# First loads under semaphores of their own, and a last stage in column halves of 290, in a one-core adapter, attention and expert kernel

## Time and profile before

| | us |
|---|---|
| median of 3 runs | 1396.19 (1395.92 to 1399.05) |
| the profiled execution | 1395.68 |
| its span in the profile | 1393.9 |
| TensorE busy in the span | 1328.4 (95%) |
| VectorE busy | 1068.3 (77%) |
| ScalarE busy | 861.1 (62%) |
| GpSimd busy | 655.9 (47%) |

### The profile page before, as it was taken

The page is one execution under the profiler, slowest core; times in us unless marked ns, Lnnn a source line. Parts: engine busy times, 40 slices in busy tenths (PEclk is TensorE's granted clock), DMA queues, the critical chain, the costliest instruction groups (busy, mean ns, idle before and its releaser), DMA issues.

```text
span 1393.9 us, 26480 instructions
## 1 busy us (share of the span) xinstructions
PE 1328.4 (95%) x8088; PEld 1138.0 (82%) x8088; DVE 1068.3 (77%) x2951; ACT 861.1 (62%) x2499; POOL 655.9 (47%) x652
## 2 busy tenths in 40 slices
PE   4889997799999999999999999999999999999988
PEld 3666665588888888888888888888888888888877
DVE  3677866478888888888888888888888888888855
ACT  1567776466666676666666666676666667666631
POOL 1345546453545363536453654365345535453511
PEclk9799998999999999999999999999999999999999
DMA  7445444444121212121212122312212121213121
GB/s 259 146 149 159 158 153 140 134 114 114 31 66 37 80 32 62 31 77 32 61 32 77 31 61 41 82 40 51 71 38 61 32 76 32 61 31 73 28 74 61
DMA packets 193520, 107.59 MB, mean 77 GB/s; under 512 B 140897, under 2 KB 178274, under 8 KB 191970
## 3 DMA queue, kind: packets, MB, share of 16 engines
q1 hardware_dynamic: 192224, 105.38, 28.1%
q10 hardware_dynamic: 1154, 0.50, 0.1%
HBM read 101.66 MB, written 37.75 MB: 100 GB/s over the span
## 4 chain that ended last, share of the span: by engine, by line
PE 81%; SPq 10%; DVE 3%; issue 3%; DMA 2%; ACT 1%; POOL 0%; DVEq 0%; ACTq 0%; POOLq 0%
PE ps L1168 11%; PE ps L1170 11%; PE ps L1169 11%; PE ps L1219 10%; PE ps L1240 5%; PE ps L1233 5%; PE ps L1234 5%; SPq L79 5%; PE ps L1253 4%; SPq L80 4%; PE ps L1252 4%; PE ps L1259 4%; PE ps L1195 2%; PE ps L236 1%; PE ps L892 1%
## 5 line engine op out<-in xcount | busy, mean ns | idle before, releaser
L1365 ACT ACTIVATE b_pf<-b_sm,b_nb,b_rstd 128x640 f32<-128x640 f32 x256 | 235.2, 919 | 102.4 <-DVE b_nb L1470 102.2
L1371 ACT ACTIVATE b_p_h<-ps 128x640 fp32r<-128x640 f32 x256 | 180.3, 704 | 180.3 <-PE ps L1219 179.6
L1484 DVE TENSOR_TENSOR b_p_l<-ps,b_p_h 128x640 fp32r<-128x640 f32 x256 | 210.7, 823 | 82.9 <-ACT b_p_h L1371 75.8
L1463 DVE CUSTOM_DVE_ANT_0 b_sm<-ps,mask_row 128x640 f32<-128x640 f32 x256 | 209.3, 817 | 2.7 <-PE ps L1170 2.0
L1219 PE MATMUL ps<-ident,b_pf 128*128 128x128 f32 x1280 | 182.8, 274 | 10.0 <-DVE b_p_l L1484 8.0
L1479 DVE TENSOR_SCALAR b_pf<-b_pf,b_ri 128x640 f32<-128x640 f32 x256 | 159.0, 621 | 27.7 <-DVE b_ri L1476 0.5
L1168 PE MATMUL ps<-b_w_h,x1t_h 128*128 128x512 f32 (+1 forms) x512 | 179.2, 350 | 0.5 <-DVE b_qt_l L1451 0.5
L1219 PEld LDWEIGHTS ps<-ident,b_pf 128*128 128x128 f32 x1280 | 152.9, 141 | 29.6 <-issue 10.1
L1168 PE MATMUL ps<-b_kt_h,b_qt_h 128*128 128x320 f32 x512 | 174.6, 341 | 1.0 <-DVE b_mx L1463 1.0
L1169 PE MATMUL ps<-b_w_l,x1t_h 128*128 128x512 f32 (+1 forms) x512 | 173.4, 339 | 0.0
L1170 PE MATMUL ps<-b_w_h,x1t_l 128*128 128x512 f32 (+1 forms) x512 | 172.8, 337 | 0.0
(11 more groups left out here) (163 smaller groups left out, 3237.0 us busy)
## 6 DMA issues: line engine op xcount, KB each, us to landing
kv_of_batch<-in_kv SPq DMA_DIRECT2D x128, 256.0 KB
b_ck<-kv_of_batch SPq DMA_DIRECT2D x64, 256.0 KB, 3.6
b_cv<-kv_of_batch SPq DMA_DIRECT2D x256, 64.0 KB, 2.2
raw<-in_w SPq DMA_DIRECT2D x32, 384.0 KB, 5.4
raw<-in_wo SPq DMA_DIRECT2D x32, 256.0 KB, 3.6
a_xt<-in_xt SPq DMA_DIRECT2D x8, 256.0 KB, 5.1
a_xin<-in_x SPq DMA_DIRECT2D x8, 256.0 KB, 5.2
x<-a_x SPq DMA_DIRECT2D x8, 256.0 KB, 5.2
```

The costliest lines, as they stand in the source:

```text
L1365: act.activation(pf[:, h % 2], sm[:, h % 2], ACT.Exp, bias=nb[:, m.b % 2, h:h + 1], scale=rstd[:, m.b % 4, h:h + 1], accum_out=rs[:, m.b % ...
L1371: act.activation(p_h[:, :, h * P:(h + 1) * P], turned_row, ACT.Copy).then_inc(ph_sb, 1)
L1463: dve.tensor_tensor_reduce(sm[:, h % 2], score_row, mask_row[:, m.b], 1.0, MASKED, ALU.add, ALU.max, mx[:, k, h:h + 1]).then_inc(mx_sb, 1)
L1484: dve.tensor_tensor(p_l[:, :, cols], turned_row, p_h[:, :, cols], ALU.subtract).then_inc(pl_sb, 1)
```

## The change

At the start: `la`, `lb`, `b_cond` and four column blocks of 128 of `wc` have semaphores of their own, and low_rank(0), cond(0) and y_out(0) wait for what they read. `wq` is loaded as its first 512 columns (with the small arrays, under `qkv_in`) and its last 256 (`kv_in`). ScalarE's queue issues the inputs of the choice first, then runs a small activation on zeros into `scrap`, then issues `pages` and the tables' inputs. `key_row` moves to SyncE's queue, behind `wq`'s last columns. The eight mask rows leave `table_angles`: four are made between kv_out(0) and rope_sum(0), four after `table_products` in slot 0.

In the last stage: `W3 = 580` columns are cut at `CUT = 290`. `gate(b)` makes columns 290 to 579: 222 output columns and the 68 of gate and `low`. `rest(b)` makes columns 0 to 289. `add_low_rank` writes all 512 output columns in the outputs' bank, in two pairs (290 and 222 columns). VectorE gets `add_second`, which adds the 222 columns to `hacc`, and does `low_rest(b-1)` ahead of `choose(b)`. The turned `h` has one bank, 6, and the turned `low` has bank 7. `turn(1)` and ScalarE's `h_out(1)` move behind rest(0) and `high(end, 3)`.

The diff, cut to its core:

```diff
             load(0)
-            for part, signal in ((cond_weights, cond_in), (qkv_weights, qkv_in), (rest, rest_in)):
-                for dst, name in part:
-                    sp.dma_start(dst[:], t[name]).then_inc(signal, 16)
+            sp.dma_start(la[:], t["la"]).then_inc(la_in, 16)
+            sp.dma_start(lb[:], t["lb"]).then_inc(lb_in, 16)
+            for o in range(KT):
+                cols = slice(o * P, (o + 1) * P)
+                sp.dma_start(wc[:, :, cols], t["wc"][:, :, cols]).then_inc(wc_in[o], 16)
+            sp.dma_start(b_cond[:], t["b_cond"]).then_inc(b_cond_in, 16)
+            sp.dma_start(wq[:, :, 0:D], t["wq"][:, :, 0:D]).then_inc(qkv_in, 16)
+            for dst, name in qkv_small:
+                sp.dma_start(dst[:], t[name]).then_inc(qkv_in, 16)
+            sp.dma_start(wq[:, :, D:], t["wq"][:, :, D:]).then_inc(kv_in, 16)
+            load_key_row(sp)
+            for dst, name in rest:
+                sp.dma_start(dst[:], t[name]).then_inc(rest_in, 16)
...
                 if a == 0:
-                    pe.wait_ge(cond_in, 16 * len(cond_weights))
+                    pe.wait_ge(la_in, 16)
...
+                if a == 0:
+                    pe.wait_ge(lb_in, 16)
                 for o in range(KT):
+                    if a == 0:
+                        pe.wait_ge(wc_in[o], 16)
...
-            act.dma_start(pages[:], t["pages"]).then_inc(ids_in, 16)
             for dst, name in choice:
                 act.dma_start(dst[:], t[name]).then_inc(adapters_in, 16)
+            act.wait_ge(zero_sb, 1)
+            act.activation(scrap[:], vz[:, 0, 0], ACT.Copy)
+            act.dma_start(pages[:], t["pages"]).then_inc(ids_in, 16)
             load_tables(act)
...
                 if inside(b + 1):
                     kv_out(b + 1)
+                if b == -1:
+                    table_masks(dve, range(4))
...
                 if b == 0:
                     table_products(dve)
+                    table_masks(dve, range(4, B))
...
+    def table_masks(dve, batches):
+
+        dve.wait_ge(key_row_in, 16)
+        for b in batches:
             dve.tensor_scalar(mask_row[:, b], key_row[:], lenf[:, b:b + 1], MASKED, ALU.is_ge, ALU.mult)
...
-    gate_of = lambda b: ps[:, GL[b % 3], 0:NX]
-    lowt_of = lambda b: ps[:, GL[b % 3], P:2 * P]
+    first_of = lambda b: ps[:, F[b % 3], 0:CUT]
+    second_of = lambda b: ps[:, GL[b % 3], 0:CUT]
+    gate_of = lambda b: ps[:, GL[b % 3], D - CUT:CUT]
+    lowt_of = lambda b: ps[:, LT, 0:P]
     rows_of = lambda b: ps[:, F[b % 3], :]
-    HT = (6, 7)
+    HT, LT = 6, 7
...
-        product(pe, b, gate_of(b), slice(D, W3), True).then_inc(gl_ps, 1)
+        product(pe, b, second_of(b), slice(CUT, W3), True).then_inc(gl_ps, 1)
...
-        product(pe, b, rows_of(b), slice(0, D), False).then_inc(f_ps, 1)
+        product(pe, b, first_of(b), slice(0, CUT), False).then_inc(f_ps, 1)
...
-        pe.matmul(rows_of(b), lowt[:, b % 2], bt_h, start=False, stop=False)
-        pe.matmul(rows_of(b), lowt[:, b % 2], bt_l, start=False, stop=True).then_inc(done_ps, 1)
+        for cols in (slice(0, CUT), slice(CUT, D)):
+            pe.matmul(rows_of(b)[:, cols], lowt[:, b % 2], bt_h[:, cols], start=False, stop=False)
+            mm = pe.matmul(rows_of(b)[:, cols], lowt[:, b % 2], bt_l[:, cols], start=False, stop=cols.stop == D)
+        mm.then_inc(done_ps, 1)
...
         turn(pe, 0)
-        turn(pe, 1)
...
         rest(pe, 0)
+        turn(pe, 1)
...
+    def add_second(dve, b):
+        dve.wait_ge(xb_sb, b + 1)
+        dve.tensor_tensor(hacc[:, b, CUT:], second_of(b)[:, 0:D - CUT], hacc[:, b, CUT:], ALU.add)
...
     def rows_dve(dve):
+        add_second(dve, 0)
         for b in range(1, B):
+            low_rest(dve, b - 1)
             choose(dve, b)
...
+            add_second(dve, b)
+            finish(dve, b - 1)
...
             h_out(act, 0)
+            high(end, 3)
             h_out(act, 1)
-            high(end, 3)
             split_b(act)
```

More of the change, by code:

```diff
@@ L95, in phase1 @@
         wq = sb("wq", [P, KT, QKV1])
-        load_tables, table_angles, table_products, table_sines = tables(nc, ctx, memory, t, consts)
+        load_tables, load_key_row, table_angles, table_masks, table_products, table_sines = tables(nc, ctx, memory, t, consts)
         b_qkv = sb("b_qkv", [P, QKV1])
@@ L131, in phase1 @@
         ri = sb("ri", [P, H1])
-        cond_in, qkv_in, rest_in, ids_in = sem("cond_in"), sem("qkv_in"), sem("rest_in"), sem("ids_in")
+        scrap = sb("scrap", [P, 2 * D1])
+        la_in, lb_in, b_cond_in, kv_in = sem("la_in"), sem("lb_in"), sem("b_cond_in"), sem("kv_in")
+        wc_in = [sem(f"wc_in{o}") for o in range(KT)]
+        qkv_in, rest_in, ids_in = sem("qkv_in"), sem("rest_in"), sem("ids_in")
         adapters_in, id_sb, chosen_sb = sem("adapters_in"), sem("id_sb"), sem("chosen_sb")
@@ L156, in context_bank @@
             return M2 if inside(b + 2) else M0
-        cond_weights = ((la, "la"), (wc, "wc"), (lb, "lb"), (b_cond, "b_cond"))
         choice = ((adapters, "adapters"), (ls, "ls"), (which, "which"))
-        qkv_weights = ((wq, "wq"), (b_qkv, "b_qkv"), (cos, "cos"), (sin, "sin"), (ident, "ident"))
+        qkv_small = ((b_qkv, "b_qkv"), (cos, "cos"), (sin, "sin"), (ident, "ident"))
+        QKV_LOADS = 1 + len(qkv_small)
         rest = ((blocks, "blocks"), (causal, "causal"), (wd, "wd"), (b_dense, "b_dense"))
@@ L231, in project_q @@
                 if a == 0:
-                    pe.wait_ge(qkv_in, 16 * len(qkv_weights))
+                    pe.wait_ge(qkv_in, 16 * QKV_LOADS)
                 pe.wait_ge(yt_sb, a + 1)
@@ L239, in project_kv @@
             def project_kv(a):
+                if a == 0:
+                    pe.wait_ge(kv_in, 16)
                 pe.wait_ge(yt_sb, a + 1)
@@ L389, in y_out @@
                 if a == 0:
-                    act.wait_ge(cond_in, 16 * len(cond_weights))
+                    act.wait_ge(b_cond_in, 16)
                 act.wait_ge(yt_ps, a + 1)
@@ L509, in q_out @@
                 if a == 0:
-                    dve.wait_ge(qkv_in, 16 * len(qkv_weights))
+                    dve.wait_ge(qkv_in, 16 * QKV_LOADS)
                 dve.wait_ge(q_ps, a + 1)
@@ L708, in run_gpsimd @@
             pool.wait_ge(zero_sb, 1)
-            pool.wait_ge(qkv_in, 16 * len(qkv_weights))
+            pool.wait_ge(qkv_in, 16 * QKV_LOADS)
             slots(slot)
@@ L735, in tables @@
     cosine = sb("cosine", [P, B, HD // 2])
-    loaded, step, sines = sem("loaded"), sem("step"), sem("sines")
-    loads = ((lens, "lens"), (token, "token"), (inv, "inv"), (norms, "norms"), (key_row, "key_row"))
+    loaded, step, sines, key_row_in = sem("loaded"), sem("step"), sem("sines"), sem("key_row_in")
+    loads = ((lens, "lens"), (token, "token"), (inv, "inv"), (norms, "norms"))
     def load_tables(act):
@@ L741, in load_tables, with load_key_row @@
             act.dma_start(dst[:], t[name]).then_inc(loaded, 16)
+    def load_key_row(sp):
+        sp.dma_start(key_row[:], t["key_row"]).then_inc(key_row_in, 16)
     done = [0]
@@ L763, in table_angles @@
         then(dve, dve.tensor_scalar(angle[:], angle[:], 3.1415925, -3.1415925, ALU.min, ALU.max))
-        for b in range(B):
+    def table_masks(dve, batches):
+        dve.wait_ge(key_row_in, 16)
+        for b in batches:
             dve.tensor_scalar(mask_row[:, b], key_row[:], lenf[:, b:b + 1], MASKED, ALU.is_ge, ALU.mult)
@@ L785, in table_sines @@
         act.activation(half_sine[:], angle[:], ACT.Sin, scale=0.5).then_inc(sines, 1)
-    return load_tables, table_angles, table_products, table_sines
+    return load_tables, load_key_row, table_angles, table_masks, table_products, table_sines
 def phase2_consts(nc, ctx):
@@ L881, in turn @@
     def turn(pe, b):
-        wait(pe, htl_sb, b - 1)
+        wait(pe, htl_sb, b)
         pe.wait_ge(h_sb, DONE - B + b + 1)
         for i in range(KT):
-            mm = pe.transpose(ps[:, HT[b % 2], i * P:(i + 1) * P], hacc[:, b, i * P:(i + 1) * P], ident[:])
+            mm = pe.transpose(ps[:, HT, i * P:(i + 1) * P], hacc[:, b, i * P:(i + 1) * P], ident[:])
         mm.then_inc(ht_ps, 1)
@@ L956, in h_out @@
         wait(act, f_ps, b - 1)
-        act.activation(flat(ht_h[b % 2]), ps[:, HT[b % 2], :], ACT.Copy).then_inc(hth_sb, 1)
+        act.activation(flat(ht_h[b % 2]), ps[:, HT, :], ACT.Copy).then_inc(hth_sb, 1)
     def low_out(act, b):
@@ L975, in h_rest @@
         dve.wait_ge(hth_sb, b + 1)
-        dve.tensor_tensor(flat(ht_l[b % 2]), ps[:, HT[b % 2], :], flat(ht_h[b % 2]), ALU.subtract).then_inc(htl_sb, 1)
+        dve.tensor_tensor(flat(ht_l[b % 2]), ps[:, HT, :], flat(ht_h[b % 2]), ALU.subtract).then_inc(htl_sb, 1)
     def choose(dve, b):
```

8 lines of the change are left out of this document (1 added, 7 removed).

## The result

| | before | changed kernel |
|---|---|---|
| median of the runs taken together | 1396.59 us (4 runs) | 1388.17 us (4 runs, 1387.24 to 1389.66) |
| ratio, 95% interval | | 0.9939 (0.9927 to 0.9952) |
| the profiled execution | 1395.68 us | 1389.66 us |
| its span | 1393.9 us | 1387.9 us |

8.4 us faster, inside the predicted range (1381.5 to 1390.5) and 3.6 us above the number. Five more executions of the same kernel, run later beside other experiments, gave a median of 1387.05 and a ratio of 0.9935 (0.9922 to 0.9949); over all nine executions the median is 1387.65.

What follows compares the result with a forecast made beforehand. Phase 1 was taken as bound by SyncE's queue with 0.8 us of slack, after a latency-bound start, and the last stage by TensorE. 1395.68 - 4.25 - 6.8 = 1384.6 us; own range 1382 to 1387, 80% range 1381.5 to 1390.5.

Steps and rivals of the forecast that it cites:

- rival B: Start: SyncE's issues stall behind more packets, `xt`(1) leaves at 21 or later; start gives only -0.5, 1388.4 us; chance 0.22.
- D: Last stage: the 222-column products or VectorE's order cost about 0.5 us a batch, 1388.6 us; chance 0.10.
- low_rank(0) waits for `la` and `xt` alone: 11.2 to 5.1: Start, TensorE: low_rank(0) no longer waits for `b_cond`, the last of four loads; 6.1 us gained.
- cond(0) starts at 7.7: Start, TensorE: with y_out it takes 7.6 us, `wc` blocks landing in time; project_q ready at about 15.3.
- half of the 3.79 for eight: Start, VectorE: four masks between kv_out(0) and rope_sum(0), hidden by GpSimd's 3.1 us rope; at most 1.9 if uncovered.
- The other four: Slot 0, VectorE: four masks behind table_products stand in the chain; ScalarE and TensorE wait, a full +1.9 us.
- rival C: Start: TensorE gains little, through late `which`, `wc` blocks in series or longer lower clock behind L780; 1386.4 us; chance 0.12.
- SyncE's queue ... an end at about 17.9: Start: 23 loads issued instead of 18, ending at 17.9 instead of 13.8; `xt`(1) leaves 3.4 us earlier.
- Smaller of 5.3 and 4.25: Start: TensorE reaches cond(3)'s end 5.3 us earlier, SyncE's queue gains 4.25; the smaller counts, -4.25 us.
- Last stage "-6.8": Last stage: even 290-column steps give -7.35 over eight batches, turn(1) +0.44, the tail +0.2; sum -6.8 us.
- E: Both ends give little: 0 at the start and lost time by VectorE in the last stage, 1392.7 us; chance 0.06.
- F: SyncE's queue: issues cost by the packet, `xt`(1) leaves 30 us late, kernel slower at 1418 us; chance 0.03.

Runs made afterwards that it cites:

- again: The changed kernel run once more, unaltered, beside other experiments: median 1387.05 us.
- start_only: The changed kernel with the last stage of the kernel before, so only the start is changed: 1393.38 us, ratio 0.9975 to the kernel before.
- both_again: Second run of the changed kernel with all eight masks made behind the tables' angles and turn(1) ahead of gate(0): 1385.83 us, ratio 0.9919.

## Why the prediction was right, and where its steps were off

**Range and direction** were right: both ends give, most of it the last stage. The number was not: 1388.17 lies above the forecast's own range of 1382 to 1387, and beside the 1388.4 of rival B and the 1388.6 of D, neither of whose mechanisms came. It is inside the stated range because that was drawn over the rivals. The steps, one by one:

- *"low_rank(0) waits for `la` and `xt` alone: 11.2 to 5.1"*. It was 6.0: `la` took 4.48 from issue to landing instead of 3.6. With the new start it took 4.4 to 5.0 in all eleven profiles, with the old one 3.6, 4.8 and 3.6, so the forecast rested on a quick one of three; why it varies was not tried. 0.9 was lost here.
- *"cond(0) starts at 7.7 ... some 6.2 of them its own"*. It started at 8.63 and took 7.3 (8.63 to 15.93). The first steps were slow for longer: its four blocks took 2.08, 1.71, 1.31 and 0.89 us for 8 steps, and before 2.07, 1.22, 0.89 and 0.89. Another 1.1 lost, a part of it by chance: cond(0) took 6.5 in `again`, 6.1 in start_only and 7.7 in both_again. `which` (6.1 instead of 5.3) and the first block of `wc` (7.9 instead of 7) came some 0.9 later than forecast and still in time, and the table load was hidden: 7.4 less 0.9 and 1.1 is the 5.36 that project_q gained, where 7.2 was forecast.
- *"half of the 3.79 for eight ..., hidden by GpSimd's rope"*. This is the step that failed by its kind: a cover was assumed that was not there. The four masks under the rope took 4.32 us, not 1.9, and pushed rope_sum(0) out by about 0.9 us. The rope wasn't their cover; the two engines stood in each other's way.
- *"The other four ... a full +1.9"*. 1.85 in the chain. But with them the way was 0.8 longer still, of which 0.5 can be read as the lower clock under project_q(2); the forecast had that only in rival C.
- *"SyncE's queue ... an end at about 17.9"* and *"Smaller of 5.3 and 4.25"*. The queue ended at 15.0, stalls of `raw` 2.11 instead of 4.09, and `xt`(1) left at 16.01, when TensorE let it. At the third `xt` SyncE was ready at 96.3 instead of 101.85, 5.5 earlier. TensorE arrived 1.71 earlier: -5.36, +0.9 under the rope, +1.85, and +0.9 that is left and goes with the clock. So the smaller of the two was TensorE's, the other way round from the forecast, and the sum kept a term of 4.25 that in this profile was 1.71. start_only's 3.5 by the ratio lies between.
- *Last stage "-6.8"*. A step of 290 columns took 0.135 (0.132 forecast), 222 columns 0.105 to 0.11, the period 4.26 (4.2), and no low-rank wait or VectorE order showed. The idle time before low_rest was 0.72, and the end behind gate(7) was 4.3 (4.5). At full clock the stage gave 6.29. In the profiled execution the clock took 1.53 of that. It is the clock of rival C in a place that no rival named.

Rivals B, D, E and F are out: the queue was early, the narrow steps cost their columns, issues didn't grow with packets. What came true was the forecast's mechanism with a piece of rival C, a longer low clock behind the masks.

The missing 5.05 us of the profiled execution (forecast 11.05, measured 6.0) are 2.54 at the start, 2.04 in the last stage and 0.47 in between. Over all fourteen profiles the way from the third `xt` to part 3's first values varied from 176.1 to 177.8 us, in code that none of the edits touches, so a forecast to 1 us was not to be had from one execution.

## What to carry to other kernels

When two queues must both be early, work out each one's time at the point where they meet, and mistrust the one whose terms you call hidden: here the queue with the uncertain stalls was early and the engine with the "covered" work was late. Work put under another engine's work is not free until a row shows the pair side by side; look first for idle time in which nothing runs beside it, as before q_out(0). And when a busy engine's idle time is filled less than before (a turn moved out of a seam), look at the clock in the stretch behind, in more than one execution.

## What the runs showed of the hardware

- The same mask instruction took 0.55 us alone, 1.82 us beside GpSimd's first rope product, ending 0.35 us after it, and 1.14 beside the two shorter ones; the products grew too, 1.53 to 1.67 and 0.85 to 1.09. The Trainium skill (SBUF — State Buffer, Who interferes with whom) states that VectorE in certain fast modes and GpSimd take one port pair in turns, each for a whole instruction. The long mask agrees with that; which mode the mask runs in no run here shows.
- TensorE's lower clock cost 1.53 us in four of eight last stages with the same code at the seam. In the first 120 us it lasted 23.9 us in one execution of the changed kernel and 27.3 in another.
- The first 24 steps of cond(0) took 0.26, 0.21 and 0.16 us (2.08, 1.71 and 1.31 for 8) instead of 0.11, and the granted clock reads 1.00 there, in the kernel before too. Eight such steps took 1.99 us at 36.14, where it reads 0.50, so the first ones went at the pace of the lower level. Whether that is what slowed them stays open.
